# First expert layer: six of sixteen steps of a matrix iteration as a chain ahead of the experts, ten beside them

## The reference

```python
def experts(x, Wg, w1, w2):            # E = 16, F = 512, capacity C = 4096 / 16 = 256
    gate = softmax(xr @ Wg); idx = argmax(gate)
    loc = position of the token among those of its expert; valid = loc < C
    dispatched[idx, loc] = xr
    h = relu(einsum('ecm,emf->ecf', dispatched, w1))
    out = einsum('ecf,efm->ecm', h, w2)
    return out[idx, loc] * gate[idx] * valid

def scan_matrix(W_scan_raw):           # 128 x 128
    U, _, Vt = svd(W_scan_raw)
    return U @ Vt                      # the orthogonal factor
```

## Time and profile before

| | |
|---|---|
| median of 3 runs | 1735.6 us (1734.5 to 1736.95) |
| profiled execution | 1737.16 us, its span 1735.4 us |
| TensorE busy | 1547.9 us, 89% of the span |
| VectorE, ScalarE, GpSimd busy | 78%, 55%, 37% |
| granted TensorE clock, mean | 0.941 |
| first expert layer, about | 878 to 1027 us of the span |

### The profile page before, as it was taken

One profiled execution on the slowest core, in us unless ns is written; L12 is line 12 of the kernel. 1 busy time (PEld: TensorE's weight loads), 2 busy tenths in 40 slices (PEclk: granted clock), 3 DMA queues, 4 the chain that ended last, 5 costly groups with the idle time before them and its releaser, 6 DMA issues. The chain is left out here.

```text
span 1735.4 us, 37728 instructions
## 1 busy us (share of the span) xinstructions
PE 1547.9 (89%) x13802; PEld 1017.8 (59%) x13802; DVE 1358.0 (78%) x2469; ACT 957.1 (55%) x2389; POOL 645.8 (37%) x592
## 2 busy tenths in 40 slices
PE   5699999999999999999984957999999999996486
PEld 3333333333333333333364856999999999996475
DVE  6789999999999999999553434698888888886633
ACT  4268888888888888888821324344444444442121
POOL 5300000000000000000034422888888888882634
PEclk9789999999999999999966987999999999998688
DMA  3320000000000000000073021011111222112520
GB/s 114 111 71 19 26 27 27 19 23 27 27 26 16 25 27 27 27 15 27 8 203 95 24 73 49 14 49 48 49 48 48 49 48 48 44 40 66 176 74 24
DMA packets 88407, 84.94 MB, mean 49 GB/s; under 512 B 12556, under 2 KB 74121, under 8 KB 88272
## 3 DMA queue, kind: packets, MB, share of 16 engines
q1 hardware_dynamic: 84176, 75.00, 15.5%
q0 software_dynamic: 4096, 8.13, 1.3%
HBM read 36.78 MB, written 23.59 MB: 35 GB/s over the span
## 5 line engine op out<-in xcount | busy, mean ns | idle before, releaser
L653 DVE TENSOR_REDUCE chunk_max<-ps_max 128x1 f32<-128x512 f32 (+3 forms) x1280 | 695.0, 604 | 72.4 <-PE ps_max L757 49.8
L707 ACT ACTIVATE probs<-ps_s 128x512 f32<-128x512 f32 (+3 forms) x1280 | 602.1, 533 | 152.6 <-PE ps_s L749 128.6
L1338 POOL TENSOR_TENSOR lane_products<-L,q 128x1024 f32<-128x1024 f32 x176 | 411.7, 2373 | 124.7 <-DMA L<-ident_rows 70.0
L740 PE MATMUL ps_max<-Ks,Qs 48*128 48x512 bf16 (+3 forms) x1280 | 378.9, 358 | 10.4 <-DMA Ks<-k_parts 9.6
L730 PE MATMUL ps_s<-Qs,Ks 50*128 50x512 bf16 (+3 forms) x1280 | 368.5, 350 | 11.0 <-DVE chunk_max L653 5.4
L804 PE MATMUL ps_o<-probs,Vp 128*32 128x512 f32 (+3 forms) x2560 | 340.8, 558 | 3.1 <-ACT O_sb L684 0.4
L730 PEld LDWEIGHTS ps_s<-Qs,Ks 50*128 50x128 bf16 x1280 | 111.8, 93 | 352.8 <-DVE chunk_max L653 321.7
L599 POOL TENSOR_TENSOR neg_max_b<-neg_max,no_max 128x8 bf16<-128x8 f32 x64 | 12.8, 200 | 515.2 <-DVE neg_max L638 515.2
L1644 DVE TENSOR_TENSOR weighted<-exp_scores,psV_s 128x2048 f32<-128x2048 f32 x88 | 197.0, 2280 | 0.0
L1735 PE MATMUL psZT<-ident,weighted 128*128 128x128 f32 x1408 | 167.3, 274 | 1.8 <-DVE weighted L1644 1.8
L1735 PEld LDWEIGHTS psZT<-ident,weighted 128*128 128x128 f32 x1408 | 158.1, 142 | 2.0 <-DVE weighted L1644 2.0
(11 more groups left out here) (234 smaller groups left out, 2263.4 us busy)
## 6 DMA issues: line engine op xcount, KB each, us to landing
m_w<-in_L_ffn_w_dram SPq DMA_DIRECT2D x24, 512.0 KB, 7.0
L<-q SPq DMA_DIRECT2D x16, 448.0 KB
Qs<-q_parts SPq DMA_DIRECT2D x192, 32.0 KB
Ks<-k_parts SPq DMA_DIRECT2D x192, 32.0 KB
dispatched<-blank SPq DMA_DIRECT2D x32, 132.0 KB, 2.4
L<-q SPq DMA_DIRECT2D x20, 192.0 KB
m_d<-dispatched SPq DMA_DIRECT2D x14, 264.0 KB, 4.7
L<-q SPq DMA_DIRECT2D x28, 128.0 KB
```

What stands on the lines that cost most here:

```text
L653: nc.vector.tensor_reduce(out, scores[:, 0:w], axis=AX.X, op=ALU.max).then_inc(max_reduced, 1)
L707: nc.scalar.activation(dst, ps_s[(k + r) % R][:, q0:], ACT.Exp, scale=SCALE).then_inc(exp_done, 1)
L740: last = nc.tensor.matmul(ps_max[(k + r) % R][:, 0:w], Q[r][rows, i * P:(i + 1) * P], K[r][rows, ck * QW:ck * QW + w], start=True, stop=no ...
L1338: return nc.gpsimd.tensor_tensor(c.lane_products[ch % 2][:, l].rearrange("p (j m) d -> p j m d", m=LANES), c.L[ch][:, :, l * W_LANE:(l + 1 ...
```

## The change

`early` is 6 where there are steps. Steps 0 to 5 are issued one behind the other, on TensorE behind its wait for the four quarters' `slots_ready`, on ScalarE behind the last quarter's exponentials, on VectorE behind the last quarter's slots and ahead of the first normalise. The first two `turn`s wait until the six are copied. Steps 6 to 15 lie in `up(0)` to `up(9)` as before, and `up(10)` to `up(15)` hold none. The second layer's program is unchanged.

```diff
--- before.py
+++ after.py
@@ -867,6 +867,8 @@
     CQ = NCH // QUARTERS
     S2 = CAP // P
     FT = F // P
+    early = 6 if polar_steps else 0
+    beside_experts = range(early, len(polar_steps))
     with ExitStack() as cx:
         def sb(n, shape, dt=fp32):
             return cx.enter_context(nc.sbuf_tensor(f"{name}_{n}", shape, dt))
@@ -1086,6 +1088,8 @@
                 nc.vector.scalar_tensor_tensor(out=Y_pol, in0=polar_ps[i % 2][:, 0:D], scalar=a2, in1=Z_pol,
                                                op0=ALU.mult, op1=ALU.add).then_inc(Y_done, 1)
 
+            for i in range(early):
+                polar(i)
             for e in range(3):
                 normalise(e)
             for e in range(E_):
@@ -1094,13 +1098,13 @@
                     dve.wait_ge(y_sent[u], e // 2 * 32)
                 nc.vector.tensor_copy(to_row[u][:], d_sb[:, e * S2:(e + 1) * S2, IDENTITY]).then_inc(ids_done, 1)
                 if e == 0:
-                    polar(0)
+                    polar(early)
                 dve.wait_ge(h_in_psum, e * 2 + 2)
                 nc.vector.tensor_scalar(hT[u][:, FT // 2:, :].rearrange("p f s -> p (f s)"), psH[u][:, F:], 0.0, None,
                                         ALU.max).then_inc(h_dve, 1)
                 if e + 3 < E_:
                     normalise(e + 3)
-                polar(e + 1)
+                polar(early + e + 1)
                 dve.wait_ge(y_in_psum, e + 1)
                 for s in range(S2):
                     own, gate = d_sb[:, e * S2 + s, 0:D], d_sb[:, e * S2 + s, GATE:GATE + 1]
@@ -1149,24 +1153,33 @@
                     act.wait_ge(h_in_psum, e * 2 - 2)
                 nc.scalar.activation(dT[e % 2], psD[e % 2][:, 0:CAP], ACT.Copy).then_inc(d_copied, 1)
 
+            def copy_square(i):
+                act.wait_ge(A_in_psum, i + 1)
+                nc.scalar.activation(A_pol, polar_ps[i % 2][:, 0:D], ACT.Copy).then_inc(A_copied, 1)
+
+            def copy_pair(i):
+                act.wait_ge(S_in_psum, i + 1)
+                nc.scalar.activation(c.S[:].rearrange("p a d -> p (a d)"), polar_ps[i % 2], ACT.Copy).then_inc(S_copied, 1)
+
+            for i in range(early):
+                copy_square(i)
+                copy_pair(i)
             copy_rows(0)
             copy_rows(1)
             for e in range(E_):
+                i = early + e
                 if e and e + 1 < E_:
                     copy_rows(e + 1)
-                if e < len(polar_steps):
-                    act.wait_ge(A_in_psum, e + 1)
-                    nc.scalar.activation(A_pol, polar_ps[e % 2][:, 0:D], ACT.Copy).then_inc(A_copied, 1)
+                if i in beside_experts:
+                    copy_square(i)
                 act.wait_ge(h_in_psum, e * 2 + 1)
                 if e >= 2:
                     act.wait_ge(y_in_psum, e - 1)
                 nc.scalar.activation(hT[e % 2][:, 0:FT // 2, :].rearrange("p f s -> p (f s)"), psH[e % 2][:, 0:F],
                                      ACT.Relu)\
                   .then_inc(h_act, 1)
-                if e < len(polar_steps):
-                    act.wait_ge(S_in_psum, e + 1)
-                    nc.scalar.activation(c.S[:].rearrange("p a d -> p (a d)"), polar_ps[e % 2], ACT.Copy)\
-                      .then_inc(S_copied, 1)
+                if i in beside_experts:
+                    copy_pair(i)
 
         @block.tensor
         def _(pe):
@@ -1217,12 +1230,33 @@
                 count(q)
             pe.wait_ge(slots_ready, 2 * QUARTERS)
 
+            def square(i):
+                wait(pe, S_copied, i)
+                nc.tensor.matmul(polar_ps[i % 2][:, 0:D], c.S[:, 0, :], c.S[:, 0, :], start=True, stop=True)\
+                  .then_inc(A_in_psum, 1)
+
+            def square_again(i):
+                pe.wait_ge(A_copied, i + 1)
+                nc.tensor.matmul(polar_ps[i % 2][:, 0:D], A_pol, A_pol, start=True, stop=True).then_inc(AA_in_psum, 1)
+
+            def next_pair(i):
+                pe.wait_ge(Y_done, i + 1)
+                nc.tensor.matmul(polar_ps[i % 2][:, 0:D], c.S[:, 1, :], Y_pol, start=True, stop=True)
+                nc.tensor.matmul(polar_ps[i % 2][:, D:], Y_pol, c.S[:, 1, :], start=True, stop=True).then_inc(S_in_psum, 1)
+
+            for i in range(early):
+                square(i)
+                square_again(i)
+                next_pair(i)
+
             def turn(e):
+                if e < 2:
+                    wait(pe, S_copied, early)
                 pe.wait_ge(xs_ready, e + 1)
                 if e >= 2:
                     pe.wait_ge(d_copied, e - 1)
-                    if e - 2 < len(polar_steps):
-                        pe.wait_ge(S_copied, e - 1)
+                    if early + e - 2 in beside_experts:
+                        pe.wait_ge(S_copied, early + e - 1)
                 for s in range(S2):
                     last = nc.tensor.transpose(psD[e % 2][:, s * P:(s + 1) * P], xs[e % 3][:, s, :], c.ident[:])
                 last.then_inc(d_in_psum, 1)
@@ -1232,25 +1266,19 @@
                 if e >= 2:
                     pe.wait_ge(h_act, e - 1)
                     pe.wait_ge(h_dve, e - 1)
-                if e < len(polar_steps):
-                    wait(pe, S_copied, e)
-                    nc.tensor.matmul(polar_ps[e % 2][:, 0:D], c.S[:, 0, :], c.S[:, 0, :], start=True, stop=True)\
-                      .then_inc(A_in_psum, 1)
+                i = early + e
+                if i in beside_experts:
+                    square(i)
                 own = c.w1[:, e, :] if e < KEPT else w1_sb[:, e - KEPT, :]
                 for f in range(FT):
-                    if f == FT // 2 and e < len(polar_steps):
-                        pe.wait_ge(A_copied, e + 1)
-                        nc.tensor.matmul(polar_ps[e % 2][:, 0:D], A_pol, A_pol, start=True, stop=True)\
-                          .then_inc(AA_in_psum, 1)
+                    if f == FT // 2 and i in beside_experts:
+                        square_again(i)
                     last = nc.tensor.matmul(psH[e % 2][:, f * CAP:(f + 1) * CAP], own[:, f * P:(f + 1) * P],
                                             dT[e % 2], start=True, stop=True)
                     if f % 2:
                         last.then_inc(h_in_psum, 1)
-                if e < len(polar_steps):
-                    pe.wait_ge(Y_done, e + 1)
-                    nc.tensor.matmul(polar_ps[e % 2][:, 0:D], c.S[:, 1, :], Y_pol, start=True, stop=True)
-                    nc.tensor.matmul(polar_ps[e % 2][:, D:], Y_pol, c.S[:, 1, :], start=True, stop=True)\
-                      .then_inc(S_in_psum, 1)
+                if i in beside_experts:
+                    next_pair(i)
 
             def down(e):
                 pe.wait_ge(h_act, e + 1)
```

## The result

The changed kernel takes 1739.6 us (median of 15 runs, 1738.2 to 1744.7), the kernel before in the same runs 1736.0. The ratio is 1.0027, 95% interval 1.0019 to 1.0036, so 4.7 us slower, between 3.3 and 6.2; the two medians are 3.6 apart. Predicted were 1739.6 and +4.0. Eleven of the 15 executions took 1738.2 to 1741.1 us, four took 1743.6 to 1744.7, with a mean granted clock of 0.936 to 0.939 in place of 0.941 to 0.944.

What follows compares the result with a forecast made beforehand. The hand-over gap was taken as set by GpSimd's scatters and a DMA round trip, the experts behind it by TensorE. +8.5 for the late start less 4.5 gained gives +4.0 on 1735.6: 1739.6 us, range 1735.0 to 1742.6.

Steps and rivals of the forecast that it cites:

- The window: First expert layer, last slots ready until TensorE's first weight load at 938.58: chain work there is free for 15.9 us.
- The step: One chained step without overlap: 4.08 us at the low clock, 2.99 at the high; six take 24.5 or 17.9.
- The start: The experts' first transposes wait for the six chained steps, which end at 947.1, 8.5 us late.
- Contention: Between the chain and GpSimd's scatters beside it, costed at nothing.
- The clock: TensorE in the chain: begins at the low level, 0.50, and the chain does not lift it.
- Rival A: The chain warms the clock, so the experts start at the high level: -3.4 us, 1732.2; chance 0.09.
- Rival B: Clock stays low, but a chained step costs about the warm 2.99 us: -2.5 us, 1733.1; chance 0.06.
- moved, not removed: The experts' start at the low clock, 4.6 us, comes later behind the chain but stays.
- The gain: Expert 8's second product to the last one's end: 4.45 us less, with half the last product's clock loss counted.
- the 7.5: Upper bound in us of the gain in the last six experts, with no wait for landings at all.
- Rival C: Cold chain, but the last experts gain 5.8 to 7.5 us: +1.0 to +2.7, some 1737.5; chance 0.20.
- D: Waits for landings cut the last experts' gain to 2.0 to 3.5 us: +5.0 to +6.5, some 1741; chance 0.18.

Runs made afterwards that it cites:

- early3: Changed kernel with three steps in the chain and thirteen beside the experts; ratio to the kernel before 0.9992, 1.4 us faster, in no clear way.
- ten_steps: Kernel before with only ten of the sixteen steps, beside experts 0 to 9, and no chain; ratio 0.9963, median 1731.4 us.
- early4: Changed kernel with four steps in the chain and twelve beside the experts; ratio to the kernel before 0.9989, 1.9 us faster.
- chain_added: Changed kernel with 22 steps, six as the chain and sixteen beside the experts; ratio to the kernel before 1.0050, 8.7 us slower.
- fill_ahead: Changed kernel with six added products of 512 columns on TensorE ahead of the chain; a single execution, 1739.3 us.
- filled_chain: Changed kernel with six unread 512-column products ahead of the chain and a short one in each step's three gaps; 1730.7 us, ratio to before 0.9965.
- four_rows: Changed kernel with four buffers and semaphores in place of two for to_row and y, both expert layers; ratio to the kernel before 0.9978.
- the halves: Two runs: the kernel before without the last six steps (ratio 0.9963), and the changed kernel with all sixteen kept beside the experts (1.0050).
- the runs with stalls: Later runs: kernel before with 22 added products (0.9987); filled_chain joined with four_rows, six steps (0.9989, repeat 0.9988) or five (0.9982).

## Why the prediction was right

- The window, 15.9 us: 15.99 in the kernel before, 15.0 in early3, 16.2 in ten_steps, 16.9 in early4; in none of them does a chain hold the transposes up. It is not a fixed length: it ends about 5.3 us behind the last scatter, and that one starts 9.6 to 11.6 us behind the last slots, in the changed kernel 10.3. So the 8.3 us against the profile of before are 8.8 against this execution's own scatters, and 9.4 in chain_added. The prediction took the window of one execution for all.
- The step, 4.08 at the low clock by rows of single products at that clock: 4.04. Two small misses nearly cancel: the pair took 1.26 for 1.22, ScalarE's hand-overs 0.05 for 0.08 and 0.12. The six, 24.5: 24.3. The start, 8.5 late: 8.3, and 24.27 again in chain_added. Contention, taken at nothing, shows in no step: they take 4.03 or 4.04 beside the scatters.
- The clock. The chain ran at 0.50 throughout, as read from the stretches that had stayed low. fill_ahead went further than the argument: the chain did not even hold the high level. Rival A needed a rise within two steps, and there was none. The Trainium skill says ("TensorE: Matmul & The Clock Gate", Part 1) that activity releases the throttle. Here 24 us of a chain that kept TensorE busy for 70% by the records did not release it, so the sentence alone does not decide such a case.
- Rival B, a lone product that hardly feels the clock: 0.84 against 0.52 us, 4.04 against 2.91 for a step. Refuted by the step itself and by filled_chain. The Trainium skill's figures for one bf16 product ("TensorE: Matmul & The Clock Gate", Part 2, "Single matmul latency"), 289 and 219 ns at 128 columns, give 0.28 us for the four products of a step, as an estimate from that page. The steps of fp32 products measured here differ by 1.1 us between the levels.
- The experts' cold start "moved, not removed": moved, and 0.65 longer in this execution (9.83 against 9.18), since the clock rose about 6 us behind the first transposes and not 4.6. In chain_added it was 8.77. That term was given as nothing; where the start is cold it ranges from 8.76 to 9.90 over the profiles.
- The gain, 4.45: 4.33 in this execution, by the same stretch. Right in its mechanism (four_rows removes the landings, and all of the 7.5 comes) and in its uncertainty: in ten_steps it was 5.6, where the last product ran at the high level. Counting half of the clock's loss was a middle between two outcomes that both occur. The reason given, that the clock falls because the gap is 2.15 us, does not hold: in early3 and fill_ahead the gap was 2.13 and 2.12 and the clock stayed up. The turns without a step were foreseen at 3.7 to 4.2; one took 4.47 and one 3.59. Rival C's gain, with the two buffers kept, came near in ten_steps, D's did not come.
- Sum: 8.3 + 0.65 - 4.33 = +4.6 from the gate, +4.7 (3.3 to 6.2) in time, +4.0 predicted. That it comes so near is in part luck. The profile is of one of the four long executions, and has 2.3 us at the low clock that the halves' profiles lack, 1.1 at the start and 1.2 at the end; whether the eleven shorter executions have them is not shown. The mechanism, a chain that overruns the scatters by over 8 us against a gain of 4 to 6 at the end, is shown by the two halves.

## What to carry to other kernels

A chain of dependent small products laid in an engine's idle stretch costs nothing up to the end of that stretch and its full latency beyond it; so price a step at the clock that the stretch grants, divide the stretch by it, and move no more steps than that (here four of 4.04 us in 16 us, not six). TensorE's idle stretches can be filled with products that nobody reads: that held the clock up, made the chain's step 2.91 us, and gave 2 us at the start of the work behind it, but in the runs with stalls the clock fell in spite of it. When work is taken out of the bounding engine, look in a sister stage without that work for the next bound; here that was the landing of scatters behind two buffers, and four buffers gave 8.5 us over the two layers.

## What was not expected of the hardware

The clock fell in the middle of a chain that kept TensorE busy for 3.33 of 5.30 us at the high level (fill_ahead). Three added products in each step, 0.39 to 0.49 us each, did not lengthen it: 2.91 us with them and without. Most landings take 2.2 us, the longest 3.4, and with two buffers one turn of a layer can be 0.5 to 0.7 us longer for it (4.47 in the changed kernel, with a wait of 0.93 for the landing). At which clock the last product of a layer runs, 2.02 or 3.22 us, is not settled by the gap before it. These are the last products of early3 and of fill_ahead, to set beside the changed kernel's 3.22 behind a gap of 2.12:

```profile
1021.23 2.02 PE L1290 MATMUL m_psY<-m_w,front 128*128 128x128 f32 x16 [2.13 <-issue]
...
1025.17 2.02 PE L1296 MATMUL m_psY<-m_w,front 128*128 128x128 f32 x16 [2.12 <-issue]
```

What settles it was not found. And the same two chips ran the same kernel 20 us slower at a later time; the programs profiled then had ScalarE waiting for something outside of the core's engines for 30 us in the two routing stages.
